# Third stage in two couples of lanes, half a section apart, each with its attention in four PSUM banks of its own

## The reference

```python
# L2 attention: 16 heads of 8, causal, 256 tokens
dot = einsum('bqhd,bkhd->bhqk', q, k); attn = softmax(where(causal, dot, -inf)); out = einsum('bhqk,bkhd->bqhd', attn, v)
# L2 MLP
h = gelu(x @ w1 + b1, approximate=False); h @ w2 + b2
# L3: scan, MLP, attention, MLP
n = rms_norm(xm); value, gate = split(n @ in_proj_w); value = silu(conv4(value))
y = selective_scan(value, A, x @ B_proj_w, x @ C_proj_w, dt, 64) + D * value
xm = xm + scale * (y * silu(gate) @ out_proj_w); xm = xm + scale * mlp(rms_norm(xm))      # mlp: relu squared
q, k = rms_norm of each head of 8, then rope; 16 query heads, 4 key heads; causal softmax attention
xa = xa + scale * (att @ o_w); xa = xa + scale * mlp(rms_norm(xa))
```

## Time and profile before

| | us |
|---|---|
| median of 3 runs | 3795.07 (3793.33 to 3798.79) |
| the profiled execution | 3797.36 |
| its span, first to last instruction | 3795.6 |
| TensorE busy | 2975.8 (78%) |
| VectorE busy | 2390.8 (63%) |
| ScalarE busy | 1816.6 (48%) |
| GpSimd busy | 516.4 (14%) |
| mean granted TensorE clock | 0.868 of full |

### The profile page before, as it was taken

How to read it: one execution, slowest core, us unless ns; L and a number is a source line. 1 busy time by engine, 2 the same in 40 slices (tenths; PEclk the granted TensorE clock), 3 DMA queues, 4 the chain that set the end, 5 groups by cost and what they waited for, 6 DMA issues and landing times.

```text
span 3795.6 us, 76097 instructions
## 1 busy us (share of the span) xinstructions
PE 2975.8 (78%) x31950; PEld 2354.3 (62%) x31950; DVE 2390.8 (63%) x6446; ACT 1816.6 (48%) x3876; POOL 516.4 (14%) x643
## 2 busy tenths in 40 slices
PE   6788887778888758778884887967778798686885
PEld 3466665456666547667774765856666486574564
DVE  4655555565554578888897666467565845755337
ACT  3556555555555467777773443324434332343222
POOL 1110001120100132222222011120010202002000
PEclk7889988888998879898997988987989899697887
DMA  2000000000000010000000000000000000001000
GB/s 86 1 1 1 1 1 1 1 1 1 1 1 1 1 51 6 7 9 6 7 1 12 2 2 1 2 1 2 2 1 3 1 2 1 1 3 45 1 1 23
DMA packets 13542, 27.99 MB, mean 7 GB/s; under 512 B 784, under 2 KB 9232, under 8 KB 12688
## 3 DMA queue, kind: packets, MB, share of 16 engines
q1 hardware_dynamic: 13200, 23.12, 1.8%
HBM read 21.02 MB, written 2.10 MB: 6 GB/s over the span
## 4 chain that ended last, share of the span: by engine, by line
PE 50%; DVE 36%; ACT 10%; issue 3%; POOL 1%; DMA 0%; SPq 0%; DVEq 0%; POOLq 0%; ACTq 0%
PE ps L331 6%; DVE LN L1944 5%; PE ps L322 4%; PE ps L1822 3%; PE ps L1303 3%; DVE RS L237 3%; PE ps L388 3%; PE ps L296 3%; PE ps L475 3%; DVE M L491 2%; DVE LN L1957 2%; ACT LN L268 2%; PE ps L1314 2%; DVE LN L258 2%; PE ps L1766 1%
## 5 line engine op out<-in xcount | busy, mean ns | idle before, releaser
L304 ACT COPY LN<-ps 128x512 f32<-128x512 f32 (+4 forms) x592 | 303.3, 546 | 629.4 <-PE ps L296 172.2
L283 POOL TENSOR_TENSOR RS<-RS,MISC 128x4 f32<-128x4 f32 x216 | 219.2, 1015 | 2177.2 <-DVE RS L249 1642.6
L296 PE MATMUL ps<-cons,LN 128*128 128x128 f32 x672 | 143.2, 356 | 349.7 <-DVE LN L256 124.8
L296 PEld LDWEIGHTS ps<-cons,LN 128*128 128x128 f32 x672 | 97.8, 178 | 403.7 <-DVE LN L256 143.9
L491 DVE TENSOR_REDUCE M<-ps 128x6 f32<-128x768 f32 x256 | 242.0, 955 | 140.1 <-PE ps L475 95.7
L1944 DVE TENSOR_TENSOR LN<-LN 128x1024 f32<-128x1024 f32 (+2 forms) x192 | 220.3, 1147 | 27.8 <-ACT LN L304 16.9
L388 PE MATMUL ps<-LN 32*128 32x256 f32 x1024 | 187.4, 440 | 53.3 <-DVE LN L527 32.1
L632 DVE TENSOR_REDUCE M<-ps 128x12 f32<-128x1536 f32 x64 | 112.4, 1756 | 175.2 <-PE ps L378 175.2
L322 PE MATMUL ps<-LN,wAB 128*128 128x512 f32 x384 | 207.1, 672 | 14.3 <-ACT LN L341 8.5
L1822 PE MATMUL ps<-LN,wAB 128*128 128x128 f32 x1024 | 150.9, 310 | 74.3 <-ACT LN L304 73.8
L391 PE MATMUL ps<-LN 32*128 32x256 f32 x1024 | 202.9, 475 | 0.8 <-DVE M L491 0.8
(11 more groups left out here) (345 smaller groups left out, 7563.3 us busy)
## 6 DMA issues: line engine op xcount, KB each, us to landing
wAB<-wb SPq DMA_DIRECT2D x16, 256.0 KB, 2.7
LN<-wd SPq DMA_DIRECT2D x8, 512.0 KB, 6.9
wAB<-wa SPq DMA_DIRECT2D x1, 3840.0 KB, 16.1
wCs<-wc SPq DMA_DIRECT2D x1, 2336.0 KB, 10.7
XA<-xin SPq DMA_DIRECT2D x8, 256.0 KB, 7.6
y<-XA SPq DMA_DIRECT2D x8, 256.0 KB, 2.3
wAB<-wb SPq DMA_DIRECT2D x1, 1024.0 KB, 5.0
wAB<-wm SPq DMA_DIRECT2D x1, 1024.0 KB, 4.8
```

Of the source, the lines that this page charges most:

```text
L283: pool.e.tensor_tensor(c.r[:, 40:44], c.r[:, 36:40], mhalf, ALU.pow).then_inc(*c.G.inc((k, "rstd")))
L296: ins = pe.e.transpose(ps[:, n * 128:(n + 1) * 128], src[:, n, :], ident)
L304: act.e.copy(dst, ps).then_inc(*c.A.inc(named(k, done)))
```

## The change

The four lanes become two couples (lanes 0 and 1, lanes 2 and 3). Each couple runs the nine sections on its own, with attention over its own 16 quads, own semaphores, own space for maxima, outputs and exponentials. The second couple starts 52 rounds after the first. Within a couple the lag is 3 rounds. The round counts of a lane are fixed: `l2_in` 4, `mid` 53, `l3_out` 6. An attention section has t from -5 to 19, so 25 values and 50 rounds, one half step to a round.

A couple's attention has the four banks of its lanes: 4n and 4n+1 by query, 4n+2 and 4n+3 by key, the same ones for first and second half steps.

The reciprocal square root for the queries and keys of L3 is a power -0.5 on GpSimd over 128x80 (the Sqrt on ScalarE and the reciprocal on VectorE go).

`dve_out` before phase 3 is for the first four groups alone. The others' follows in the first attention of couple 0, a piece after each "first" half step. For this the mixture's last accumulation writes to another place (`YF`).

```diff
-LAG2, LAG3 = 9, 1
+LAG3, START3 = 3, (0, 52)
+ROUNDS3 = {"l2_in": 4, "mid": 53, "l3_out": 6}
...
+class Couple:
+    def __init__(self, n, ls, signals, rl):
+        self.n, self.ls, self.rl = n, ls, rl
+        self.P, self.A, self.D = signals
+        self.q0, self.k0 = 4 * n, 4 * n + 2
...
+    def pt(self, s, h):
+        return self.pts[s % 3][h].rearrange("p (j c) -> p j c", j=2)
...
+def abreast(gens, lag):
+    live, rnd = dict(enumerate(gens)), 0
+    while live:
+        for n in sorted(live):
+            if rnd >= lag * n:
+                try:
+                    next(live[n])
+                except StopIteration:
+                    del live[n]
+        if live:
+            yield
+        rnd += 1
...
-            by_key = [] if qt is None else [(j, 4 + j) for j in (2 * h, 2 * h + 1)]
-            by_query = [] if qs is None else [(j, j) for j in (2 - 2 * h, 3 - 2 * h)]
+            by_key = [] if qt is None else [(2 * h + i, cp.k0 + i) for i in range(2)]
+            by_query = [] if qs is None else [(2 - 2 * h + i, cp.q0 + i) for i in range(2)]
...
                 if qt is not None or w is not None:
-                    for i in (6, 7):
-                        banks.fill(pe, i, A4, (k, t, "second"))
+                    for i in range(2):
+                        banks.fill(pe, cp.k0 + i, A, (k, t, "second"))
                 if qs is not None or wt is not None:
-                    for i in (0, 1):
-                        banks.fill(pe, i, D4, (k, t, "second"))
+                    for i in range(2):
+                        banks.fill(pe, cp.q0 + i, D, (k, t, "second"))
...
-                D4.mark((k, t, "first"))
+                D.mark((k, t, "first"))
+                next(side, None)
+                yield
...
-            dve.wait_ge(c.A, (k, "rms"))
-            dve.e.reciprocal(rb, rb).then_inc(*c.D.inc())
+            dve.wait_ge(c.G, (k, "rms"))
...
-            act.wait_ge(c.D, (k, "ms"))
-            act.e.activation(v["rb"], v["rb"], ACT.Sqrt).then_inc(*c.A.inc((k, "rms")))
...
             pool_values(pool, c, k, views23(c))
-            yield from idle(5)
+            yield from idle(2)
+            rb = views23(c)["rb"]
+            pool.wait_ge(c.D, (k, "ms"))
+            pool.e.tensor_tensor(rb, rb, mhalf[:, 0:1].to_broadcast([128, 80]), ALU.pow).then_inc(*c.G.inc((k, "rms")))
+            yield from idle(3)
...
-                        ins = dve.e.scalar_tensor_tensor(YA[:, b, m, :], YA[:, b, m, :], al[:, b:b + 1],
+                        dst = YF if q == 15 else YA
+                        ins = dve.e.scalar_tensor_tensor(dst[:, b, m, :], YA[:, b, m, :], al[:, b:b + 1],
...
+        def dve_out_later(dve, ls):
+            for c in ls:
+                yield from dve_out(dve, c, c.n + 4)
+                yield
...
-        def phase3(eng, ls, l2_in, mid, l3_out, attend):
+        def phase3(eng, cps, l2_in, mid, l3_out, attend):
+            def lane(c, items):
+                for name, make, half in items:
+                    yield from paced(make(eng, c, 4 * half + c.n), ROUNDS3[name])
+            def stage(cp, *items):
+                yield from abreast([lane(c, items) for c in cp.ls], LAG3)
+            def couple(cp):
+                yield from stage(cp, ("l2_in", l2_in, 0))
+                yield from attend(cp, ("l2", 0))
+                yield from stage(cp, ("mid", mid, 0))
+                yield from attend(cp, ("l3", 0))
+                yield from stage(cp, ("l3_out", l3_out, 0), ("l2_in", l2_in, 1))
+                yield from attend(cp, ("l2", 1))
+                yield from stage(cp, ("mid", mid, 1))
+                yield from attend(cp, ("l3", 1))
+                yield from stage(cp, ("l3_out", l3_out, 1))
+            together([couple(cp) for cp in cps], start=START3)
...
-            run_lanes(dve_out, dve, 1)
+            together([dve_out(dve, c, c.n) for c in lanes()], 1)
...
+            def attend(cp, ka):
+                if cp.n == 0 and ka == ("l2", 0):
+                    for c in lanes():
+                        for _ in pool_out(pool, c, c.n + 4):
+                            pass
+                yield from idle(2 * (16 + 9))
```

More of the change, by code:

```diff
@@ L149, in together, with paced @@
         rnd += 1
+def abreast(gens, lag):
[10 more added lines that the diff above has]
+        rnd += 1
+def paced(gen, rounds):
+    for n in range(rounds):
+        next(gen, None)
+        yield
+    for _ in gen:
+        raise ValueError("more rounds than planned")
 def v4(ps):
@@ L219, in lanes1, with couples @@
                     for n in range(LANES)]
+        couple_signals = [[Signal(sem(f"{name}{n}"), tables.setdefault(f"{name}{n}", {})) for name in
+                           ("pe_attend", "act_attend", "dve_attend")] for n in range(2)]
+        def couples(banks=None):
+            ls = lanes(banks)
+            return [Couple(n, ls[2 * n:2 * n + 2], couple_signals[n], MISC[:, 196:212] if n == 0 else MISC[:, 120:136])
+                    for n in range(2)]
         def sync_all(eng, key):
@@ L528, in dve_attend, with act_attend @@
                                                   RL[:, :, :, i:i + 1].to_broadcast([128, 2, 4, q.d]), ALU.mult)
[L529 to L534, removed]
+                    ins.then_inc(*D.inc((k, w, "values")))
+                D.mark((k, t, "second"))
+                yield
+        def act_attend(act, cp, k, quads, nb, nw):
+            n, A, P = len(quads), cp.A, cp.P
+            for t in range(-nb - 1, n + 4):
@@ L541, in act_attend @@
                     q = quads[t - 4]
                     o = 1536 + 256 * q.b
[L543 to L548, removed]
+                    act.e.copy(q.c.M[:, o:o + 256].rearrange("p (t c) -> p t c", t=2), spare(cp.k0)).then_inc(
+                        *A.inc((k, on, "on")))
@@ L556, in views01 @@
+                A.mark((k, t, "second"))
+                yield
         def views01(c):
@@ L2326, in phase1 @@
             together([lane(c) for c in ls], start=START1)
-        def phase3(eng, ls, l2_in, mid, l3_out, attend):
-            def stage(eng, c, item):
-                half, make = item
-                yield from make(eng, c, 4 * half + c.n)
-            for step, ka in (([(0, l2_in)], ("l2", 0)), ([(0, mid)], ("l3", 0)), ([(0, l3_out), (1, l2_in)], ("l2", 1)),
-                             ([(1, mid)], ("l3", 1)), ([(1, l3_out)], None)):
-                together([chain(stage, eng, c, step) for c in ls], LAG3)
-                if ka is not None and attend is not None:
-                    attend(ka, quads23(ls, ka), 4, 2)
+        def phase3(eng, cps, l2_in, mid, l3_out, attend):
[15 more added lines that the diff above has]
+            together([couple(cp) for cp in cps], start=START3)
         def pe_program(e):
@@ L2364, in pe_program @@
             banks = Banks()
-            phase3(pe, lanes(banks), pe_l2_in, pe_mid, pe_l3_out, attend)
+            phase3(pe, couples(banks), pe_l2_in, pe_mid, pe_l3_out, attend)
             ended(PD, "p3")
@@ L2415, in dve_program, with attend @@
             dve.e.memset(ON1, 0.0).then_inc(*DD[LANES].inc())
-            def attend(ka, quads, nb, nw):
-                dve_attend(dve, ka, quads, nb, nw)
+            def attend(cp, ka):
+                later = dve_out_later(dve, lanes()) if cp.n == 0 and ka == ("l2", 0) else iter(())
+                yield from dve_attend(dve, cp, ka, quads23(cp.ls, ka), 4, 2, later)
             phase1(dve, lanes1(), dve_l0, dve_l1)
```

152 lines of the change are left out of this document (81 added, 71 removed).

## The result

| | before | after |
|---|---|---|
| median, us | 3794.2 (3786.45 to 3798.79, 4 runs) | 4132.7 (4129.66 to 4135.6, 4 runs) |
| the profiled execution | 3797.36 | 4135.6 |
| mean granted TensorE clock | 0.868 | 0.832 |

The ratio is 1.0894, with a 95% interval of 1.0874 to 1.0915: the change makes the kernel 339 us slower. The direction was forecast, the size was not: 53 us were forecast, and the time is far outside of the range.

The account below looks back on a forecast made before the run. TensorE's own work was taken as the bound in attention and scan, the chain of norms, MLP and rope elsewhere; schedule 35, power 28 and dve_out -10 made 53 us on 3797.36: 3850 us, range 3740 to 3950.

Parts of the forecast that it names:

- the mixed sections, 4x216 = 864: Phase 3, one couple's mid beside the other's attention: four sections of 216 us, where the same work took 240 before.
- The scan term: Mixed sections, the 35 rounds with a lane in the scan: 135 us of TensorE work, at 95% 142 us.
- the rounds before and after the scan: Mixed sections, chain of norms, MLP and rope: some 50 us each for two lanes, less shared and lag rounds.
- 183/0.85 = 215: Mixed sections: 183 us of TensorE work at phase 1's busy share of 85%, taken as support for 216.
- The lone attentions: Start and end of phase 3, one couple's attention alone: 145 us first, 155 last; losses of 77 and 87.
- at 1.2 GHz throughout: Rival for the lone attentions: half clock all along, 170 us instead of 145, twice; 3900 us in all, chance 0.12.
- The working of a half step: Lone attention: matmuls, then VectorE's maximum of 0.96 us and 0.1 back; a plain one 2.2 us at full clock.
- half of the clock's loss: Lone attention: 119 us at full clock, some 50 more at half clock, half of it taken: 145 us.
- The power: Reciprocal square root in mid on GpSimd, eight of 128x80: 8 us a piece, 28 us more in all.
- a charge for each column: Rival for GpSimd's power: 16.1 us a piece, 65 us above the forecast, 3915 us in all, chance 0.20.
- The middle: Phase 3, rounds 163 to 228, attention of both couples with l3_out and l2_in: 176 us of TensorE at 86%, 205 us.
- `dve_out`: End of phase 2: four groups moved save 17 us, 7 come back in the lone attention; net -10 us.

Follow-up runs that it names:

- a_sqrt: The changed kernel with the square root on ScalarE and the reciprocal on VectorE again, nothing on GpSimd: 4083.11 us, ratio 1.0761.
- a_fill: The changed kernel, square root on ScalarE, with an unused 512-column matmul after half steps of the two lone attentions up to t = 15: 4016.84 us, ratio 1.0608.
- a_start0: The changed kernel with the square root on ScalarE and both couples started in the same round: 3857.47 us, ratio 1.0166.
- b_warm: The kernel before with dve_out's second half moved and sixteen unused 128-column matmuls more for each lane in mid: 3789.48 us against 3799.14, ratio 0.9976.

## Why the prediction was right in direction and wrong in size

By its steps, with the ladder of the runs beside it: 26 us for the couples and their banks, 37 for the lag, 226 for the offset, 50 for the power. That is 339. Of the 226 the two lone attentions are 210 (58 of them the clock), the mixed sections and the middle 50, and what two lanes save in `l2_in` and `l3_out` takes some 35 off.

**The step that failed: the mixed sections, 4x216 = 864.** They were to gain 96 us against the same work before (4x240) and so pay for the lone attentions; in `a_sqrt`, without the power, they take 1044 and lose. The scan term was good: 142, and between the instructions named above 138. The mis-sized term is the rounds before and after the scan, put at "some 50 each", less 12 shared by a pair and less 10 of each for the lag, which leaves 74 us a section. They take 68 + 70 = 138 in `a_sqrt`, of which 8 are shared with the section before. Three things were wrong. Attention beside them was taken to cost nothing, and costs 30 us (138 against 108 alone). The 20 taken off for the lag did not come off. And the two-lane chain by itself is 108 and not 100. Together with the scan's -4 and the 8 shared for 6 this is the first section: 216 - 4 + 30 + 20 + 8 - 2 = 268. In the kernel after, four sections of 283, 268, 282 and 268 are 1101 us for the 892 with the power: 209 of the 285 by which the profiled execution missed 3850. Why the second section of each pair is 14 us shorter stays open.

**The figure that seemed to confirm it was a false friend.** 183/0.85 = 215 took TensorE's busy share from phase 1. There attention meets chains all along; here it met the scan. TensorE's share in the mixed sections is 74%.

**The lone attentions.** They took 182 us with `l2_in` and the moved `dve_out` where 162 were put down, and 175 for 155. The rival "at 1.2 GHz throughout" was the right case: 168 us where it gave 170, and 175 for the last. Its 50 us came true and it still missed by some 230, since the mixed sections are in it too. The working of a half step held. It gave 1.92 + 0.96 + 0.1 = 2.98 us at half clock; here is TensorE, 3.02 us apart, each time behind VectorE's maximum:

```profile
2115.29 0.80 PE L436 MATMUL ps<-LN 32*128 32x256 f32 x2 [1.15 <-DVE LN L541]
...
2118.31 0.79 PE L436 MATMUL ps<-LN 32*128 32x256 f32 x2 [1.15 <-DVE LN L541]
...
2121.33 0.79 PE L436 MATMUL ps<-LN 32*128 32x256 f32 x2 [1.15 <-DVE LN L541]
```

The choice of half of the clock's loss was wrong. It went by the stretch after the scan, where TensorE idles in long pieces at 0.75; here TensorE idled 1.15 us in every 3, and the clock was 0.58; with a matmul in the pauses (`a_fill`) it was 0.94.

**The power.** 13.1 us a piece, between the 8 taken and the 16.1 of a charge for each column; this lies nearer to the rival's. By the forecast's own formula 8x(13.1 - 4.5) is 69, which is what the kernel before paid, with 8.2 of 13.1 waited for. The kernel after paid 50, between the forecast's 28 and the rival's 93. The step was right and its size a guess, as it said.

**The middle** took 242 for 205. It takes 233 in `a_start0` too, so most of that miss is not the offset; the same kind of chain stands in its `l3_out` and `l2_in`, but no run took this stretch apart. **`dve_out`** of four groups took 21 us for 17; the step was forecast at -10 and gave -6 on its own, in the order of before. **`l2_in`** and the last **`l3_out`** were right within 6 us.

**Not forecast at all** was the lag: 3 rounds between the lanes of a couple in place of 1 cost 34 and 37 us in two pairs of runs, probably since each section ends two rounds later with fewer lanes in it. The prediction counted its rounds and gave them no time.

What stays open: how the 26 us of the couples divide between banks, fixed round counts and the rise and fall of a second attention, and through which engine the attention makes the rounds around the scan 30 us longer; VectorE's in-order stream, which both couples share, was not tested by itself.

## What to carry to other kernels

When one half's work is to fill the other's idle time, first price what the offset leaves alone at either end: one couple's attention took as long by itself as both couples' side by side, so of the 358 us of the two lone ones 210 were loss. Then lay both out by rounds and ask which rounds meet: here 35 of the filler's 50 rounds met the stretch in which TensorE was already busy 90%. A chain's time does not halve with its lanes (207 us for two, 363 for four); a time for fewer lanes has to come from the chain's own steps. And an engine that waits 1 us after each small burst may run its whole stretch at half clock, so price it there, and try a spare matmul between the bursts.

## What the runs showed of the hardware

- A power of 128x4 on GpSimd takes 1.02 us, one of 128x80 13.1 us: (13.1 - 1.02)/76 is an estimate of 0.16 us for each further column, from two sizes. A product of 128x4 takes 0.22.
- TensorE busy 63% of a stretch, in bursts with pauses of 1.15 us where they are plain, ran at a mean granted clock of 0.60 (`a_sqrt`); one further matmul in most of the pauses brought 0.94, and the stretch fell from 182 to 147 us (`a_fill`).
- Extra matmuls in the 97 us before an attention raised the clock there from 0.76 to 0.83 and left it at 0.53 in the attention's first 23 us (`b_warm`).
- A table load on ScalarE takes 1.28 us; the kernel after has 141 of them, the kernel before 133.
